# Expert biases as the last row of pivoted weights, made on GpSimd through a DRAM scratch, in place of gathered bias rows

## The reference, cut to what matters

```python
x = x + _L0_xattn_ref(_layernorm(x), ctx_768, ...)
x = x + _L0_ffn_ref(_layernorm(x), ...)
x = x + _L1_xattn_ref(_layernorm(x), ctx_768, ...)
x = x + _L1_ffn_ref(_layernorm(x), tile_sigs, W, b)
# _L1_ffn_ref:
idx = jnp.argmax(pe @ sign(tile_sigs).T, axis=-1)      # one expert per position
y_all = jnp.einsum('bsd,tod->bsto', x, W) + b          # W (8, 256, 256), b (8, 256)
out = y_all[position, idx[position]]
```

## Time and profile before

| what | us |
|---|---|
| median of 3 runs | 281.93 (280.33 to 282.77) |
| the profiled execution, whole | 282.23 |
| its span in the profile | 280.5 |
| TensorE busy | 251.9 |
| VectorE busy | 223.2 |
| ScalarE busy | 159.2 |
| GpSimd busy | 198.6 |

### The profile page before, as it was taken

How to read it: one execution, slowest core, us unless ns; L and a number is a source line. 1 busy time by engine, 2 the same in 40 slices (tenths; PEclk the granted TensorE clock), 3 DMA queues, 4 the chain that set the end, 5 groups by cost and what they waited for, 6 DMA issues and landing times.

```text
span 280.5 us, 6201 instructions
## 1 busy us (share of the span) xinstructions
PE 251.9 (90%) x2048; PEld 224.7 (80%) x2048; DVE 223.2 (80%) x566; ACT 159.2 (57%) x502; POOL 198.6 (71%) x371
## 2 busy tenths in 40 slices
PE   1777799799999999999999999999999999989860
PEld 1666566789998978999799899988799999767750
DVE  2799998999989989964998989687579679857640
ACT  3349597453575776694468777553664462464410
POOL 3529759669888975999365756888785954667664
PEclk9995999699999999999999999999999999999996
DMA  7990200201202002812000110212250000010111
GB/s 177 336 309 18 76 4 0 75 2 39 77 0 70 9 2 78 298 24 58 0 2 14 64 37 4 75 40 75 86 180 4 0 2 0 0 61 37 57 75 75
DMA packets 10957, 17.80 MB, mean 63 GB/s; under 512 B 1510, under 2 KB 7181, under 8 KB 10925
## 3 DMA queue, kind: packets, MB, share of 16 engines
q1 hardware_dynamic: 9005, 12.16, 13.7%
q0 software_dynamic: 1920, 5.25, 5.9%
HBM read 14.26 MB, written 3.15 MB: 62 GB/s over the span
## 4 chain that ended last, share of the span: by engine, by line
PE 62%; DVE 22%; issue 5%; POOL 3%; DMA 3%; ACT 2%; SPq 1%; POOLq 0%; DVEq 0%; ACTq 0%
PE PB L258 28%; PE PB L251 13%; PE S L381 4%; PE PB L458 4%; PE PB L393 4%; PE S L371 4%; PE PB L333 4%; POOL out_x L1296 2%; DVE X L742 2%; DVE SX L649 2%; DMA RT<-in_w_qr 2%; DVE SM L608 2%; DMA x<-X 1%; DVE HL L676 1%; DVE WD L831 1%
## 5 line engine op out<-in xcount | busy, mean ns | idle before, releaser
L1242 POOL TENSOR_TENSOR E<-E,SX 128x308 f32<-128x308 f32 x64 | 44.0, 716 | 10.6 <-DVE SX L666 10.6
L1050 ACT ACTIVATE E<-S,SX 128x77 f32<-128x77 f32 x128 | 39.6, 344 | 12.8 <-DVE SX L649 8.8
L258 PE MATMUL PB<-W2H,HH 128*128 128x256 f32 x128 | 37.9, 296 | 0.0
L258 PE MATMUL PB<-XTH,W1H 128*128 128x256 f32 x128 | 37.9, 296 | 0.0
L258 PE MATMUL PB<-XTL,W1H 128*128 128x256 f32 x128 | 36.2, 283 | 0.0
L258 PE MATMUL PB<-XTH,W1L 128*128 128x256 f32 x128 | 36.2, 282 | 0.0
L258 PE MATMUL PB<-W2L,HH 128*128 128x256 f32 x128 | 35.7, 279 | 0.0
L258 PE MATMUL PB<-W2H,HL 128*128 128x256 f32 x128 | 35.7, 279 | 0.0
L1073 ACT ACTIVATE HH<-PB 128x512 fp32r<-128x512 f32 x32 | 19.2, 601 | 23.2 <-PE PB L258 23.1
L1199 POOL TENSOR_TENSOR SM<-SM,nhalf 128x2 f32<-128x2 f32 x40 | 28.6, 714 | 3.1
L1050 ACT ACTIVATION_READ_ACCUMULATOR E<-S,SX 128x1 f32 x128 | 28.8, 225 | 0.0
(11 more groups left out here) (203 smaller groups left out, 725.4 us busy)
## 6 DMA issues: line engine op xcount, KB each, us to landing
RAW<-in_w SPq DMA_DIRECT2D x4, 512.0 KB, 5.5
WD<-in_WD SPq DMA_DIRECT2D x8, 256.0 KB, 4.9
X<-in_x SPq DMA_DIRECT2D x4, 256.0 KB, 7.7
x<-X SPq DMA_DIRECT2D x4, 256.0 KB, 2.1
E<-in_WD SPq DMA_DIRECT2D x4, 256.0 KB, 3.7
bc<-in_rows SPq DMA_DIRECT2D x1, 768.0 KB, 7.1
X<-in_w1r SPq DMA_DIRECT2D x1, 512.0 KB, 8.2
RT<-in_WD SPq DMA_DIRECT2D x2, 256.0 KB, 3.0
```

Of the source, the lines that this page charges most:

```text
L258: t = e.matmul(dst, a, b, start=first and j == 0, stop=last and j == n - 1)
L1050: t = e.activation(Ei[:, h * NK:(h + 1) * NK], P[:, at:at + NK], ACT.Exp, bias=SX[:, i, 0, k:k + 1], accum_out=SX[:, i, 1, k:k + 1])
L1242: t = e.tensor_tensor(Eh, Eh, SX[:, i, 2, 8 * a + h:8 * a + h + 4].unsqueeze(2).to_broadcast([128, 4, NK]), ALU.mult)
```

## The change

For stage D the kernel now does what A and B do. The input `WD` holds the experts' transposed matrices with the bias as row 255 of each, the old row 255 comes as a second input `WDr` of 8 x 256, and a row of 256 zeros as `zero`. After `f_o`, SyncE loads for each of the eight experts a block of 128 x 512 into `RAW` together with its last row broadcast to 128 partitions (twice; to 127 for the second half, whose last partition holds the zeros), GpSimd subtracts (`pivot_d`, two instructions of 128x256), and SyncE stores the block to a DRAM scratch `w3` of 2 MB. Two buffers alternate. The 15 weights are loaded from `w3` once all eight blocks are stored. D's tokens are normed over 255 columns; `oneD` sets the last one to 1.

Gone are `bs`, `bd`, `EI` with its three VectorE instructions, and `pa`'s wait for `bd`. Wq's two forms now lie in `RAW` and are loaded after `w_lo(4)`, so `gx(4)` and `gx(5)` wait no longer for `f_m` and `f_q`. Several signals are merged (`wq` with `wqr`, `sg` with `pe`, `fWk` with `fWv`, `fWqT` with `fWq`), w_q's loads are issued ahead of w_v's, `w_lo` waits for each of its instructions before the next (a signal `low`), and `r_ranks` counts on `d`. The lists of all four compute engines are planned anew.

```diff
+        w3 = nc.dram_tensor("w3", (1024, 512), F32, kind="Internal").ap()
-        FWQT, FWQ = X[:, 4, :, :], X[:, 5, :, :]
+        FWQT, FWQ, FWO = (two(RAW[:, a, o:o + 512]) for a, o in ((0, 0), (1, 0), (0, 512)))
...
             def pa(b, r):
                 w.wait_ge(s["pr"], 8 * b + r + 1)
-                w.wait_ge(s["bd"], 4 * b + min(r, 3) + 1)
...
             def w_lo(n):
                 for o in range(0, 1024 if n else 512, 256):
+                    if o:
+                        w.wait_ge(s["low"], low_made[0])
...
             def gx(g):
-                if g in (4, 5):
-                    w.wait_ge(s["p_f"], g)
...
+            def pivot_d(n):
+                w.wait_ge(s["pwz"], 32)
+                w.wait_ge(s[f"pw{n % 2}"], 48 * (n // 2 + 1))
+                W = RAW[:, n % 2, :]
+                for c in range(0, 512, 256):
+                    e.tensor_tensor(W[:, c:c + 256], W[:, c:c + 256], W[:, 512 + c:768 + c], ALU.subtract).then_inc(s["pvd"], 1)
+
+            def oneD():
+                w.wait_ge(s["p_f"], 3)
+                e.memset(XN[:, 4, :, LAST:LAST + 1], 1.0).then_inc(s["oneD"], 1)
...
-            def bd(g):
-                w.wait_ge(s["bs"], 128)
...
-            def bs(n):
-                w.wait_ge(s["ei"], 1)
-                w.wait_ge(s["p_f"], 7)
...
             # SyncE's list, after w_lo(4)
             w.wait_ge(s["wlo"], 5)
-            load("fWo", two(raw(R_WO)), chunks("Wo", 128))
+            load("fWqq", FWQT, chunks("WqT", 128))
+            load("fWqq", FWQ, chunks("Wq", 128))
+            load("fWo", FWO, chunks("Wo", 128))
+            w.wait_ge(s["p_f"], 7)
+            for n in range(2):
+                load("pwz", RAW[127:128, n, 768:1024], A["zero"])
+            for n in range(9):
+                if n < 8:
+                    if n > 1:
+                        w.wait_ge(s[f"w3{n % 2}"], 16 * (n // 2))
+                    load(f"pw{n % 2}", RAW[:, n % 2, 0:512], A["WD"][n * 128:(n + 1) * 128, :])
+                    load(f"pw{n % 2}", RAW[:, n % 2, 512:768], A["WDr"][n:n + 1, :].to_broadcast([128, 256]))
+                    load(f"pw{n % 2}", RAW[0:127, n % 2, 768:1024], A["WDr"][n:n + 1, :].to_broadcast([127, 256]))
+                if n:
+                    w.wait_ge(s["pvd"], 2 * n)
+                    load(f"w3{(n - 1) % 2}", w3[(n - 1) * 128:n * 128, :], RAW[:, (n - 1) % 2, 0:512])
             w.wait_ge(s["route2"], 1)
             load_starts(e, 0, 7 * 128, first)
-            w.wait_ge(s["ei"], 1)
-            w.wait_ge(s["p_f"], 7)
+            w.wait_ge(s["w30"], 64)
+            w.wait_ge(s["w31"], 64)
             load_weights(range(8))
```

The places of the lists that the prediction speaks of, before and after:

```diff
 VectorE
-  pivot(0); kf(); r_sign(); lo("A", 0); kbl(0); vs(); stats("A", 1); ...; ssum(0, 0, 0); r_ranks(); smax(0, 1, 1)
-  ssum(1, 1, 0); stats("B", 0); r_position(); smax(2, 0, 0); ssum(1, 1, 1); kbl(1); f_kv(0); apply("B", 0)
+  pivot(0); kf(); lo("A", 0); r_sign(); kbl(0); vs(); r_ranks(); stats("A", 1)
+  ssum(1, 1, 0); ssum(1, 1, 1); stats("B", 0); r_position(); smax(2, 0, 0); smax(2, 0, 1); apply("B", 0); f_kv(0)
-  apply("D", 4); x2(7); pa(0, 1); stats("C", 7); pa(0, 2); pa(0, 3); apply("C", 7)
+  apply("D", 4); x2(7); stats("C", 7); pa(0, 1); pa(0, 2); apply("C", 7)
 TensorE
-  pv(1, 0, 2); f_kv(0, 0); f_kv(1, 3); tE(1, 1, 1, 1); tB(0, 0)
+  sc(2, 0, 0, 1); tE(1, 1, 1, 0); pv(1, 0, 2); sc(2, 0, 1, 0); f_kv(0, 3); f_kv(1, 0)
 GpSimd
-  w_lo(0); r_iota(); bo(0); ...; f_gb(); en(1, 0, 1); en(1, 1, 0); w_lo(2); rs("B", 0); en(1, 1, 1); w_lo(3); bo(2); w_lo(4)
+  w_lo(0); r_iota(); rs("A", 1); ...; w_lo(2); en(1, 0, 0); f_gb(); ...; rs("B", 0); w_lo(3); w_lo(4); bo(1); bo(2)
+  rs("B", 3); be(2); pivot_d(0); pivot_d(1); en(4, 0, 0); en(4, 0, 1); en(4, 1, 0); be(3); b2(3); pivot_d(2)
+  bo(7); one(5); pivot_d(5); pivot_d(6); rs("C", 3); pivot_d(7); rs("B", 5); en(6, 0, 0)
```

More of the change, by code:

```diff
@@ L329, in turn @@
                     w.wait_ge(s["one"], max(g, 1) + 1)
+                elif K == "D":
+                    w.wait_ge(s["oneD"], 1)
                 P = hold(("t" + K, g), ("B", p), until)
@@ L948, in f_o @@
                                 .to_broadcast([NK, 2, 256]), ALU.add).then_inc(s["d_f"], 1)
-            setup(); mask(); stats("A", 0); apply("A", 0); pivot(0); kf(); r_sign(); lo("A", 0); kbl(0); vs()
-            stats("A", 1); ql(0); vb(0); apply("A", 1); smax(0, 0, 0); pivot(1); stats("A", 2); smax(0, 0, 1)
-            pivot(2); apply("A", 2); smax(0, 1, 0); lo("A", 1); ssum(0, 0, 0); r_ranks(); smax(0, 1, 1); ssum(0, 0, 1)
-            ssum(0, 1, 0); f_stats(); ssum(0, 1, 1); ql(1); r_expert(); lo("A", 2); smax(1, 0, 0); smax(1, 0, 1)
@@ L979, in vector @@
[L979 to L981 removed]
+            setup(); mask(); stats("A", 0); apply("A", 0); pivot(0); kf(); lo("A", 0); r_sign(); kbl(0); vs()
+            r_ranks(); stats("A", 1); ql(0); vb(0); apply("A", 1); pivot(1); smax(0, 0, 0); smax(0, 0, 1)
@@ new lines, in vector @@
+            stats("A", 2); lo("A", 1); pivot(2); smax(0, 1, 0); apply("A", 2); ssum(0, 0, 0); ssum(0, 0, 1)
+            smax(0, 1, 1); ssum(0, 1, 0); f_stats(); ssum(0, 1, 1); ql(1); r_expert(); smax(1, 0, 0); lo("A", 2)
+            smax(1, 0, 1); stats("A", 3); ssum(1, 0, 0); f_norm(); smax(1, 1, 0); ql(2); ssum(1, 0, 1); smax(1, 1, 1)
+            x1(0); ssum(1, 1, 0); ssum(1, 1, 1); stats("B", 0); r_position(); smax(2, 0, 0); smax(2, 0, 1)
+            apply("B", 0); f_kv(0); f_kv(1); ssum(2, 0, 0); ssum(2, 0, 1); smax(2, 1, 0); lo("B", 0); smax(2, 1, 1)
@@ new lines, in vector @@
+            x1(1); apply("A", 3); stats("B", 1); hl(0, 0); hl(0, 1); kbl(1); f_m(); hl(0, 2); vb(1); ssum(2, 1, 0)
+            lo("A", 3); r_index(); apply("B", 1); hl(0, 3); r_pairs(); ql(3); lo("B", 1); stats("A", 4); smax(3, 0, 0)
+            y(0); ssum(2, 1, 1); smax(3, 0, 1); ssum(3, 0, 0); hl(1, 0); hl(1, 1); stats("Y", 0); apply("A", 4)
+            hl(1, 2); x2(0); hl(1, 3); f_q(); stats("C", 0); smax(3, 1, 0); smax(3, 1, 1); f_c(); stats("A", 5)
+            stats("A", 6); ssum(3, 0, 1); apply("A", 5); ssum(3, 1, 0); lo("A", 4); ssum(3, 1, 1); x1(2)
@@ new lines, in vector @@
+            stats("B", 2); apply("C", 0); y(1); ql(4); stats("Y", 1); apply("B", 2); smax(4, 0, 0); x2(1); lo("A", 5)
+            stats("C", 1); lo("B", 2); smax(4, 0, 1); f_o(); x1(3); stats("A", 7); stats("B", 3); ql(5); ssum(4, 0, 0)
+            smax(4, 1, 0); smax(4, 1, 1); hl(2, 0); hl(2, 1); hl(2, 2); apply("B", 3); smax(5, 0, 0); ssum(4, 0, 1)
+            ssum(4, 1, 0); hl(2, 3); cm(0); lo("B", 3); starts(); apply("C", 1); ssum(4, 1, 1); y(2); stats("Y", 2)
+            hl(3, 0); ssum(5, 0, 0); hl(3, 1); hl(3, 2); apply("A", 6); smax(5, 0, 1); hl(3, 3); x2(2); smax(5, 1, 0)
@@ new lines, in gpsimd @@
+            en(3, 0, 0); be(1); rs("C", 0); rs("A", 5); one(2); en(3, 0, 1); en(3, 1, 0); en(3, 1, 1); rs("B", 2)
+            rs("A", 6); rs("Y", 1); one(3); gx(7); b2(2); rs("C", 1); rs("A", 7); rs("B", 3); be(2); pivot_d(0)
+            pivot_d(1); en(4, 0, 0); en(4, 0, 1); en(4, 1, 0); be(3); b2(3); pivot_d(2); en(4, 1, 1); bo(4)
+            en(5, 0, 0); bo(5); rs("Y", 2); pivot_d(3); pivot_d(4); rs("C", 2); bo(6); one(4); en(5, 0, 1)
+            en(5, 1, 0); en(5, 1, 1); rs("B", 4); rs("Y", 3); oneD(); bo(7); one(5); pivot_d(5); pivot_d(6)
@@ new lines, in gpsimd @@
+            rs("C", 3); pivot_d(7); rs("B", 5); en(6, 0, 0); en(6, 0, 1); en(6, 1, 0); en(6, 1, 1); b2(4); be(4)
+            be(5); rs("Y", 4); sx(1); rs("C", 4); one(6); sx(0); b2(5); en(7, 0, 0); en(7, 0, 1); en(7, 1, 0)
+            en(7, 1, 1); rs("D", 0); rs("B", 6); rs("D", 1); rs("Y", 5); sx(3); sx(2); one(7); rs("C", 5); b2(6)
+            rs("D", 2); rs("B", 7); rs("D", 3); b2(7); be(6); be(7); rs("D", 4); rs("Y", 6); rs("C", 6); rs("D", 5)
+            rs("Y", 7); rs("C", 7); put(0, 0); put(0, 1); rs("D", 6); put(0, 2); put(0, 3); rs("D", 7); put(0, 4)
@@ L1315, in sync @@
+            put(0, 5); put(0, 6); put(0, 7); put(1, 0); put(1, 1); put(1, 2); put(1, 3); put(1, 4); put(1, 5)
+            put(1, 6); put(1, 7)
         def sync(e):
@@ L1329, in load_weights @@
                 for n in which:
-                    load(f"wd{n}", weights_of(n), A["WD"][bass.ds(first[n], 128), :])
+                    load(f"wd{n}", weights_of(n), w3[bass.ds(first[n], 128), :])
             load("ldx0", X[:, 0, :, :], x_v[0])
```

250 lines of the change are left out of this document (107 added, 143 removed).

## The result

The changed kernel takes **295.74 us** (median of 4 runs, 294.03 to 296.96) beside 281.69 of the kernel before: a ratio of 1.0497 (95% interval 1.0427 to 1.0567), five per cent slower. The forecast was 278.0, so the sign was wrong, and the time lies far above the range. The profiled execution took 295.62 us, with a span of 293.6.

What follows compares the result with a forecast made beforehand. TensorE was taken to bound the middle, VectorE to set the pace of the first 60 us. Head -3.1, middle +0.5 and tail -1.5 gave -4.1 on 282.23 us, 278.1; forecast 278.0 us, range 274.0 to 283.5.

Steps and rivals of the forecast that it cites:

- the third of the four things that could stall: Middle, pivot_d: 5.2 us a block, a 6 us stall at pivot_d(7) covered by slack; +0.5 us, between 0 and +8.
- rival (2): Middle: pivot_d holds up GpSimd's list longer than the cushion, at pivot_d(7), costing 8 us, so 286 us; chance 0.16.
- f_m's wait: Middle, first possible stall: f_m waits for Wq's forms, loaded behind w_lo(4); 0 us, between 0 and +5.
- (a): Head: w_q's broadcast last row, which pivot(0) waits for, is issued one place earlier; -0.5 us, between -0.5 and 0.
- (b): Head: kbl(0)'s two instructions no longer run beside bo(0) on GpSimd; -0.6 us, between -0.6 and 0.
- (c): Head: r_ranks' three instructions move out of the time of a w_lo; -0.5 us, between -1 and 0.
- (d): Head, r_position: the 64-element product of 2.93 us no longer waits for w_lo(2)'s four GpSimd instructions; -2.0 us.
- (f): Head: TensorE's idle time ahead of f_kv shrinks and f_kv may run at full clock; -0.5 us, between -2.2 and 0.
- rival (3): Term (f)'s 2.2 us count in full and the tail closes all 2.5 us of idle TensorE time: 275 us; chance 0.10.
- (e): Head: ssum(1,1,1), a reduction and a small reciprocal, now stands ahead of r_position on VectorE; +1.0 us.
- (g): Tail: x2(7)'s pair no longer runs beside bd's additions on GpSimd; -0.8 us, between -0.9 and 0.
- (h): Tail: pa(0,1) moves behind the statistics that the last attention needs; -1.0 us, between -1.1 and 0.

Runs made afterwards that it cites:

- experiment 1: The changed kernel with the broadcast to 127 partitions issued as one to 112 and one to 15: 273.94 us, ratio 0.9708 to the kernel before.
- experiment 2: The changed kernel without the second broadcast and the zeros, both subtractions using one broadcast row: 272.16 us, ratio 0.9653 to the kernel before.
- experiment 5: The kernel of experiment 2 plus, per block, a broadcast to 126 partitions that nobody reads: 274.23 us, ratio 0.9675 to the kernel before.
- experiment 7: The kernel of experiment 2 without the waits between w_lo's instructions: 271.04 us, ratio 0.9585 to the kernel before.
- experiment 10: The kernel of experiment 2 plus, per block, a broadcast to 125 partitions that nobody reads: 273.62 us, ratio 0.9686 to the kernel before.
- experiment 11: The kernel of experiment 7 with w_v's load issued again ahead of w_q's two: 273.59 us, ratio 0.9619 to the kernel before.
- experiment 12: The kernel of experiment 2, w_lo's waits kept, with w_v's load issued again ahead of w_q's two: 273.83 us, ratio 0.9674 to the kernel before.
- experiment 4: The kernel of experiment 2 plus, per block, a broadcast to 127 partitions that nobody reads: 288.51 us, ratio 1.0175 to the kernel before.
- experiment 9: The kernel of experiment 2 plus, per block, a broadcast to 113 partitions that nobody reads: 285.04 us, ratio 1.0069 to the kernel before.
- experiment 6: The kernel before with only the changed kernel's waits between w_lo's instructions added: 282.52 us, ratio 0.9993.
- experiment 8: The kernel before without bs, bd and pa's wait, in its old lists, D's biases left out: 279.76 us, ratio 0.9898.

## Why the prediction was wrong, point by point

**The step that failed is `pivot_d`**, in the third of the four things that could stall. It took a landing of 4.9 us from a load of 128 partitions and put the third load, to 127, under the same price, where it landed 8.1 to 8.6 us behind its issue (12.8 in the second block) and held up what was issued behind it on its one engine; rival (2) even wrote of "two broadcasts of 128 rows". The buffer's turn of 10.5 us became about 20 (two blocks of 9.7 and 10.3), the block 10 us in place of 5.2. The sum gave +0.5, with 8 as the upper end, and the middle lost 21.8. Rival (2) had the chain right (GpSimd held up, TensorE behind it, then the gather) and a chance of 0.16, but its price of 8 us came from 9.1 us of landing in a full queue, and its place was `pivot_d(7)`, while TensorE already stood still at `pivot_d(1)`. One sign that the prediction named for the wrong case did appear: GpSimd idle for over 6 us ahead of a `pivot_d` (7.70 and 7.25 us), with TensorE idle later. It decided "from a landing of about 7 us on", and the load's 8.1 to 8.6 and the store's 8.3 are beyond that. The clock adds to it: 5.2 of the 21.8 us are TensorE's own work at a lower granted clock behind the stalls, and the prediction had charged idle time alone.

**What was hidden stayed hidden.** With the load repaired, the middle took 128.4 to 128.8 us in experiments 1, 2, 5, 7, 10, 11 and 12 (129.40 before), so the forecast's picture of a full TensorE that covers the pivots, w_lo's waits and the moved loads was right. GpSimd's net loss of work gave at most 1 us there, as forecast. f_m's wait is 0: Wq's form landed in 2.8 us, not 9.1. The gather waited 2.19 us in the changed kernel for x3's stores, 1.34 in experiment 1 and nothing in 2: term 0 to 1.

**The head**: -5.4 against -3.1 by these two profiles. f_o ended at 103.2 to 105.5 us, 104.3 by the mean, in the seven profiled kernels that have the changed head as it is (the changed one and experiments 1, 2, 4, 5, 9 and 10), and at 107.5 to 109.3, 108.2 by the mean, in the three with the old lists (before, 6 and 8). That is -3.9, so the forecast of the head was nearer than the table makes it look. VectorE's timeline of the changed kernel:

```profile
7.22 0.43 DVE L584 SCALAR_TENSOR_TENSOR RAW<-RT,RAW 128x256 f32<-128x256 f32 x1 [0.89 <-DMA RT<-in_w_qr]
...
12.04 0.85 DVE L766 TENSOR_TENSOR KBL<-XTE,mask 128x308 fp32r<-128x308 f32 x2
...
13.62 0.15 DVE L803 TENSOR_SCALAR WD<-WD 128x8 f32<-128x8 f32 x1
...
30.27 2.35 DVE L817 TENSOR_TENSOR WD<-WD 128x64 bf16<-128x64 f32 x1
...
44.56 0.22 DVE L831 TENSOR_TENSOR WD<-WD 128x64 f32<-128x64 f32 x1
```

- (a) The pivot starts 1.1 us earlier (8.30 to 7.22); -0.5 was forecast. In experiments 11 and 12, with the old order, it starts 0.3 and 0.7 us later than in 7 and 2; but it starts anywhere from 7.12 to 7.69 in kernels with the new order, so what the order gives is not shown.
- (b) kbl(0)'s pair takes 0.85 in place of 1.90: -1.05 for -0.6. (c) r_ranks' last instruction 0.15 in place of 0.70: as forecast.
- (d) The product takes 0.22, so -2.7 for -2.0. But one of its like in r_expert (line 817) now takes 2.35 us, beside en and w_lo, where it took 0.35 before, and a third (line 813) 0.23 in place of 0.83; the forecast had left 0.7 for such a collision. Together that is -1.3. The Trainium skill's rule ("SBUF — State Buffer", section "Who interferes with whom") limits a wait to one instruction, and the rows at 45.20 before and at 29.74 in experiment 11 go against that.
- (f) f_kv took half, and TensorE did not stand idle ahead of it. TensorE's timeline:

```profile
47.74 2.37 PE L250 MATMUL PB<-WD,XN 96*128 96x154 f32 x16
...
54.60 0.42 PE L257 MATMUL PB<-XTH,W1H 128*128 128x256 f32 x1
```

It was 4.45 us behind 2.4 us of idle time. The first feed-forward product is 4.8 us earlier (54.60 for 59.43). I had given (f) 0.5 as slack; rival (3)'s 2.2 was nearer. Experiment 6 has nearly the same gain in f_kv, though (2.34 us for 4.45), and no time less by its runs. (e), +1.0, has no row that would set it apart. How the 5.4 us divide among (b), (d), (e) and (f) was not tried one by one, and stays open.

**The tail**: -3.4 against -1.5. VectorE's timeline of the changed kernel:

```profile
255.19 0.88 DVE L697 SCALAR_TENSOR_TENSOR X<-XN,SM,X 128x256 f32<-128x256 f32 x2 [0.24 <-DVE XN L691]
257.07 1.10 DVE L743 SCALAR_TENSOR_TENSOR X<-PB,MK,X 128x256 f32 x2
```

(g) is right to 0.1 us: 0.88 for 1.76. Experiment 8 keeps the old list and takes the biases away: from the pair on it saves 2.3 us (39.5 for 41.8), so `bd` cost more than its collision with x2(7). The other 1.1 us of the 3.4 are about what (h) forecast for the new order; no run tests it alone. The last scatter began 34.4 us behind x2(7)'s start, 37.2 before.

Without the failed step the sum would have been the head's -5.4, the middle's -0.8 and the tail's -3.4, about 9.6 us down (8.1 with the head's -3.9); by the medians the repaired kernels were 8.7 (experiment 1) to 11.7 us (experiment 7) below the one before that ran beside them. So the change without this fault was worth about twice what the forecast said, and one partition too few turned its sign.
